# 72 of the 220 runs of edge rows are summed per tile inside the edge loop, the other 148 (listed as 150) in the summing pass behind it

## The reference, cut to what matters

```
h = concatenate([x[col], edge_attr], axis=1)      # col = dst, row = src
h = relu(h @ W1.T + b1)                           # 100,000 edges x 128
h = relu(h @ W2.T + b2)
summed = segment_sum(h, row, num_segments=n)      # per source node
cnt = segment_sum(ones, row, num_segments=n)
agg = summed / maximum(cnt, 1)
```

## Time and profile before

| | us |
|---|---|
| median of 3 runs | 3594.32 |
| the runs | 3587.15, 3594.32, 3613.79 |
| the profiled execution | 3586.66 |
| its span, first to last instruction | 3585.0 |
| mean granted clock of PE, share of full | 0.756 |

### The profile page before, as it was taken

One profiled execution on the slowest core, in us unless ns is written; L12 is line 12 of the kernel. 1 busy time (PEld: TensorE's weight loads), 2 busy tenths in 40 slices (PEclk: granted clock), 3 DMA queues, 4 the chain that ended last, 5 costly groups with the idle time before them and its releaser, 6 DMA issues. The chain is left out here.

```text
span 3585.0 us, 73734 instructions
## 1 busy us (share of the span) xinstructions
PE 2797.0 (78%) x15652; PEld 1906.7 (53%) x15653; DVE 2301.0 (64%) x7322; ACT 1370.4 (38%) x2945; POOL 1923.8 (54%) x1865
## 2 busy tenths in 40 slices
PE   7257777777777777545869988888898988885887
PEld 4146656665665666433333445555555555554875
DVE  7279999999999999657242235444444444443775
ACT  1045555555555555333000014444444444440001
POOL 0267777777777777530020006777777777773000
PEclk7556666656666656556879988888889788887998
DMA  4444444444444445881734322333333333334884
GB/s 138 86 122 120 136 125 115 126 127 116 120 137 113 120 119 102 70 121 52 217 104 129 109 63 69 84 82 80 82 82 81 80 82 80 82 79 132 253 256 121
DMA packets 584019, 404.72 MB, mean 113 GB/s; under 512 B 437776, under 2 KB 504643, under 8 KB 582916
## 3 DMA queue, kind: packets, MB, share of 16 engines
q1 hardware_dynamic: 449782, 133.68, 16.4%
q0 software_dynamic: 59344, 100.63, 13.9%
q10 hardware_dynamic: 74592, 167.22, 12.8%
HBM read 215.94 MB, written 210.09 MB: 119 GB/s over the span
## 5 line engine op out<-in xcount | busy, mean ns | idle before, releaser
L822 POOL DMA_INDIRECT at_hs<-table,at_rec_s x976 | 1050.3, 1076 | 409.0 <-issue 225.5
L2238 POOL DMA_INDIRECT edge_rows<-el_rows,el_idx x816 | 843.8, 1034 | 263.6 <-issue 232.0
L860 ACT CAST at_count_s<-near_ps 128x400 f16<-128x400 f32 x976 | 482.8, 495 | 754.8 <-PE near_ps L963 663.1
L963 PE MATMUL near_ps<-at_pair_hot,at_src_low_hot 128*128 128x425 f16 x976 | 477.7, 489 | 335.8 <-ACT at_count_s L860 274.7
L935 PEld LDWEIGHTS sums_ps<-at_hw,at_hit 128*128 128x128 f32 x1952 | 470.4, 332 | 34.0 <-issue 29.0
L935 PE MATMUL sums_ps<-at_hw,at_hit 128*128 128x66 f32 x1952 | 441.5, 408 | 8.4 <-DVE acc L1009 8.4
L963 PEld LDWEIGHTS near_ps<-at_pair_hot,at_src_low_hot 128*128 128x128 f16 x976 | 137.8, 141 | 444.5 <-ACT at_count_s L860 349.3
L1001 DVE TENSOR_SCALAR at_pair_hot<-iota_wide,at_rec_s 128x400 f16<-128x400 f16 x976 | 322.7, 333 | 0.1
L1009 DVE SCALAR_TENSOR_TENSOR acc<-acc,at_fade,sums_ps 128x66 f32 x976 | 266.5, 273 | 73.8 <-PE sums_ps L935 67.8
L2445 DVE TENSOR_TENSOR el_idx<-el_place,el_aside 128x8 uint32<-128x8 f32 x102 | 17.4, 171 | 454.0 <-DMA edge_rows<-el_rows,el_idx 453.7
L2522 PE MATMUL ts_sum_ps<-ts_rows,ts_hot 128*128 128x128 f32 x1760 | 221.9, 282 | 73.4 <-DVE ts_hot L2539 71.9
(11 more groups left out here) (404 smaller groups left out, 4599.9 us busy)
## 6 DMA issues: line engine op xcount, KB each, us to landing
slots<-at_count_s ACTq DMA_DIRECT2D x122, 850.0 KB
ts_rows<-edge_rows SPq DMA_DIRECT2D x110, 288.0 KB
ts_rows<-edge_rows ACTq DMA_DIRECT2D x110, 288.0 KB
el_rec<-attr SPq DMA_DIRECT2D x816, 32.0 KB
chunk<-slots SPq DMA_DIRECT2D x256, 100.0 KB
chunk<-slots ACTq DMA_DIRECT2D x208, 100.0 KB
attr<-in_edge_attr SPq DMA_DIRECT2D x16, 1248.0 KB
at_rec_s<-meta SPq DMA_DIRECT2D x976, 3.5 KB
```

The source lines that it names most:

```text
L822: pool.indirect_dma_start(hs[:, s, u, :], None, k.table, bass.IndirectOffsetOnAxis(rec[:, s, u, 0:1].bitcast(U32), 0)).then_inc(gathered[s ...
L860: a.copy(count[:, (n.o + d) % 2, i, 0:AW], near[:, (n.o + d) % 2, 0:AW]).then_inc(count_ready, 1)
L963: pe.matmul(near[:, s, 0:SW], low_hot[:, s, i, :], pair_hot[:, s, i, :], start=False, stop=True, skip_group_check=(i > 0)).then_inc(near_r ...
L2238: pool.indirect_dma_start(k.edge_rows, bass.IndirectOffsetOnAxis(idx[:, o % RECS, 4 * h + u:4 * h + u + 1], 0), rows[:, j, u, :], None).th ...
```

## The change

A unit that is full (all of its 512 rows are there) can be summed before the edge loop ends. The new code takes 72 full units (EARLY = (17 - 9 - 2) * 12) and sums them in the loop's last laps.

- After lap 8, DVE's `table()` works out from the running totals `run` how many full units each tile has, takes the first 72, and makes lists: rows of the 72 early units, and rows and tiles of the units that are left (up to 150, LATE). SP writes the six lists to DRAM and reads them back onto one partition (`quad_list`).
- In laps 10 to 15, ACT issues the loads of two early units at the end of each step (`load_quads`). One step later, DVE makes two `quad_hot` masks at its step's end (`quad_hots`); one after that PE makes the two sums, one in each half step between product1 and product2 (`sum_quads`); one after that DVE adds them to `k.sums` (`add_quads`, at its step's start, after two register reads). The pipeline drains in lap 16.
- To make room for two PSUM banks, `ea_ps` has one buffer instead of two, and PE waits for the previous half's copy before it transposes.
- `k.sums` is cleared by POOL before the edge loop's scatters instead of by DVE at the summing pass's start.
- The summing pass has 10 laps of 15 units with 6 row buffers. Since 15 is no multiple of 6 or 4, a unit's waits name the last user of its buffer in the lap before (`prior`).
- `finish_attention` no longer makes the unit lists (27 DVE steps and a memset fewer, 3 small steps more).
- The edge loop's code is written out in four laps and two hardware loops instead of two and one.

```diff
 RECS = 3
 EB = 6
-LAP = 20
-LOADS = 5
+TABLE_LAP = 9
+EARLY = (NB3 // EB - TABLE_LAP - 2) * 2 * EB
+LAP = 15
+LATE = -(-(Q2 - EARLY) // LAP) * LAP
+LOADS = 6
...
+            step(v.tensor_tensor_scan(unit_end[:], k.units[:], none[:], 0.0, ALU.add, ALU.add))
+            step(v.tensor_tensor(k.row_base[:], unit_end[:], k.units[:], ALU.subtract))
             step(v.tensor_scalar(k.row_base[:], k.row_base[:], float(UNIT), -1.0, ALU.mult, ALU.add))
             step(v.tensor_scalar(total[:], unit_end[:], -1.0, 0.0, ALU.add, ALU.max))
             step(v.tensor_scalar(total[:], total[:], float(UNIT), None, ALU.mult))
             step(v.tensor_copy(k.last_row[:], total[0:1, :]))
-            for t in range(NT):
-                step(v.scalar_tensor_tensor(tile_of[:], k.iota_wide[:, 0:Q2], unit_end[:, t:t + 1], tile_of[:], ALU.is_ge,
-                                            ALU.add))
-            step(v.tensor_copy(k.quad_tile[:], tile_of[0:1, :]))
-            step(v.tensor_scalar(tile_of[:], k.iota_wide[:, 0:Q2], float(UNIT), total[:, NT - 1:NT], ALU.mult, ALU.min))
-            step(v.tensor_copy(k.quad_row[:], tile_of[0:1, :]))
+            step(v.tensor_scalar(k.last_unit[:], unit_end[:, NT - 1:NT], -1.0, None, ALU.add))
+            for i in range(2):
+                step(v.tensor_scalar(k.iota_p2[:, i:i + 1], k.iota_p[:], float(P * i), None, ALU.add))
...
-        ea_ps = ps("ea_ps", [P, 2, CW])
+        ea_ps = ps("ea_ps", [P, CW])
...
+        quad_rows = sb("quad_rows", [P, LOADS, 4, HR])
+        quad_hot = sb("quad_hot", [P, 4, 4, P])
+        sum_ps = ps("sum_ps", [P, 2, CW])
...
+        def laps(eng, body, table=None):
+            body(0, True, False, None)
+            with eng.Fori(1, TABLE_LAP) as it:
+                body(it, False, False, None)
+            if table is not None:
+                table()
+            body(TABLE_LAP, False, False, None)
+            body(TABLE_LAP + 1, False, False, FIRST)
+            with eng.Fori(TABLE_LAP + 2, LAPS - 1) as it:
+                body(it, False, False, RUN)
+            body(LAPS - 1, False, True, DRAIN)
+
+        def slots(sums, o, lag):
+
+            if sums is None or (sums == FIRST and o < lag) or (sums == DRAIN and o >= lag):
+                return []
+            return [2 * (o - lag), 2 * (o - lag) + 1]
+
+        def nth(it, i):
+
+            return it * (2 * EB) + (i - 2 * EB * (TABLE_LAP + 1))
...
+                if not first and not last and sums is None and isinstance(it, int):
+                    sp.wait_ge(table_ready, 1)
+                    sp.dma_start(k.quad_dram.rearrange("i p -> p i"), found_i[:]).then_inc(table_written, 16)
+                    sp.wait_ge(table_written, 16)
+                    sp.dma_start(k.quad_list[:], k.quad_dram.rearrange("(a i) p -> a i p", a=1)).then_inc(list_loaded, 16)
...
+            nc.gpsimd.memset(k.sums[:], 0.0).then_inc(sums_clear, 1)
...
                 if not start:
-                    pe.wait_ge(ea_copied, q - 1)
+                    pe.wait_ge(ea_copied, q)
 
                 pe.sem_inc(passed, 1)
                 for u in range(4):
-                    t = pe.transpose(ea_ps[0:D, h, u * P:(u + 1) * P], rec[:, r, 4 * h + u, :], k.ident[:])
+                    t = pe.transpose(ea_ps[0:D, u * P:(u + 1) * P], rec[:, r, 4 * h + u, :], k.ident[:])
...
+            def sum_quads(it, some):
+
+                for i in some:
+                    pe.wait_ge(quad_hot_ready, nth(it, i + 1))
+                    if not (isinstance(it, int) and nth(it, i) < 2):
+                        pe.wait_ge(added, nth(it, i - 1))
+                    for r in range(4):
+                        m = pe.matmul(sum_ps[:, i % 2, 0:H], quad_hot[:, i % 4, r, :], quad_rows[:, i % LOADS, r, 0:H],
+                                      start=(r == 0), stop=(r == 3))
+                    m.then_inc(summed, 1)
...
                     product1(it, o, 1, now, False)
+                    due = slots(sums, o, 2)
+                    sum_quads(it, due[0:1])
                     product2(it, o, 0, start)
...
                         product1(it, o + 1, 0, now, False)
+                    sum_quads(it, due[1:2])
                     product2(it, o, 1, start)
...
+            def load_quads(it, some, at):
+
+                for i in some:
+                    if not (isinstance(it, int) and nth(it, i) < LOADS):
+                        act.wait_ge(summed, nth(it, i + 1 - LOADS))
+                        act.sem_inc(passed, 1)
+                    act.dma_start(quad_rows[:, i % LOADS].rearrange("p r f -> p (r f)"),
+                                  k.edge_rows[bass.ds(at[i], UNIT), :].rearrange("(p r) f -> p (r f)", p=P)
+                                  ).then_inc(quad_loaded[i % LOADS], 16)
+
+                if sums == FIRST:
+                    act.wait_ge(list_loaded, 16)
+                if sums in (FIRST, RUN):
+                    at = nc.values_load_multi_w_load_instructions(
+                        k.quad_list[0:1, 0, bass.ds(it * (2 * EB) - 2 * EB * (TABLE_LAP + 1), 2 * EB)],
+                        engines=[mybir.EngineType.Activation], min_val=0, max_val=JUNK - UNIT,
+                        skip_runtime_bounds_check_because="a row in front of the spare ones")[1]
...
+                    if sums in (FIRST, RUN):
+                        load_quads(it, slots(sums, o, 0), at)
...
+            def table():
+
+                step = Steps(dve, table_step)
+                step(v.memset(ones[:], 1.0))
+                step(v.memset(taken[:], 0.0))
+                step(v.tensor_tensor(count[:], run[:], k.row_base[:], ALU.subtract))
+                step(v.tensor_copy(full_i[:], count[:]))
+                step(v.tensor_single_scalar(full_i[:], full_i[:], 9, ALU.arith_shift_right))
+                step(v.tensor_copy(full[:], full_i[:]))
+                step(v.tensor_tensor_scan(ends_at[:, 0], ones[:], full[:], 0.0, ALU.mult, ALU.add))
+                step(v.tensor_tensor(count[:], ends_at[:, 0], full[:], ALU.subtract))
+                step(v.tensor_scalar(count[:], count[:], -1.0, float(EARLY), ALU.mult, ALU.add))
+                step(v.tensor_scalar(count[:], count[:], 0.0, None, ALU.max))
+                step(v.tensor_tensor(taken[:, 0:NT], count[:], full[:], ALU.min))
+                step(v.tensor_tensor(left[:], k.units[:], taken[:, 0:NT], ALU.subtract))
+                step(v.tensor_tensor_scan(ends_at[:, 0], ones[:], taken[:, 0:NT], 0.0, ALU.mult, ALU.add))
+                step(v.tensor_tensor_scan(ends_at[:, 1], ones[:], left[:], 0.0, ALU.mult, ALU.add))
+                for i, (w, c, more) in enumerate(((0, 0, left[:]), (1, 0, taken[:, 1:NT + 1]), (1, 1, taken[:, 1:NT + 1]))):
+                    at = k.iota_p2[:, c:c + 1]
+                    step(v.scalar_tensor_tensor(scrap[:], ends_at[:, w], at, ones[:], ALU.is_le, ALU.mult,
+                                                accum_out=found[:, i, 0:1]))
+                    step(v.scalar_tensor_tensor(scrap[:], ends_at[:, w], at, more, ALU.is_le, ALU.mult,
+                                                accum_out=found[:, i, 1:2]))
+                    step(v.tensor_tensor(found[:, i, 1:2], found[:, i, 1:2], at, ALU.add))
+                    if w:
+                        step(v.tensor_tensor(found[:, i, 1:2], found[:, i, 1:2], taken[:, 0:1], ALU.add))
+                step(v.tensor_tensor(found[:, :, 1], found[:, :, 1], k.last_unit[:].to_broadcast([P, 3]), ALU.min))
+                step(v.tensor_scalar(found[:, :, 1], found[:, :, 1], float(UNIT), None, ALU.mult))
+                step(v.tensor_copy(found_i[:, 0:3], found[:, :, 1]))
+                v.tensor_copy(found_i[:, 3:6], found[:, :, 0]).then_inc(table_ready, 1)
+            def quad_hots(it, some):
+                for i in some:
+                    dve.wait_ge(quad_loaded[i % LOADS], nth_load(it, i))
+                    if not (isinstance(it, int) and nth(it, i) < 4):
+                        dve.wait_ge(summed, nth(it, i - 3))
+                    v.tensor_tensor(quad_hot[:, i % 4], quad_rows[:, i % LOADS, :, H:H + 1].to_broadcast([P, 4, P]),
+                                    k.iota_row[:].unsqueeze(1).to_broadcast([P, 4, P]), ALU.is_equal).then_inc(quad_hot_ready, 1)
+            def nth_load(it, i):
+                per = 16 * (2 * EB // LOADS)
+                return it * per + (16 * (i // LOADS) + 16 - per * (TABLE_LAP + 1))
+            def add_quads(it, some, tiles):
+                for i, tile in zip(some, tiles):
+                    dve.wait_ge(summed, nth(it, i + 1))
+                    if not (isinstance(it, int) and nth(it, i) < 1):
+                        dve.wait_ge(added, nth(it, i))
+                    at = k.sums[:, bass.ds(tile, 1), :].rearrange("p t h -> p (t h)")
+                    v.tensor_tensor(at, at, sum_ps[:, i % 2, 0:H], ALU.add).then_inc(added, 1)
+            def body(it, first, last, sums):
+                if sums == FIRST:
```

(28 more changed lines are left out.)

83 lines of the change are left out of this document (50 added, 33 removed).

## The result

Measured side by side, the kernel before took 3587 to 3614 us in four executions and the changed one 3564.31 to 3576.86 us, median 3571.33 (five runs). A fifth execution of the kernel before took 3804 us, in a slower state that some executions show whatever the kernel, and is left out. The ratio is 0.9932, with a 95% interval of 0.991 to 0.9954: 0.7% faster, 24 us, where 1.7% and 60 us were forecast. The profiled execution after took 3576.86 us, with a span of 3575.2 and a mean granted clock of 0.752.

A forecast was written before the change was run, and what follows sets the result against it. POOL's scatters were taken to bound the edge loop, with the summing pass running alone after it. 3586.66 - 74 + 14 - 1 = 3526 us, and 7.7 more for the median, gave 3534 us, 1.7% faster, range 3505 to 3575.

The forecast's parts named there:

- What bounds the kernel: Edge loop: POOL's scatters bound it at 10.71 us a step; summing pass: runs alone, 257.9 us for 220 units.
- A lap is 9.7 + 8.9: Summing pass: a lap of 15 takes 18.6 us, stalled start plus nine sums; the pass 184 us, gain 74.
- 15 register reads (1.35 x 15 / 20 = 1.0): Summing pass, lap start: reading 15 tile numbers into registers costs 1.0 us plus gaps, scaled from 1.35 for 20.
- The clock: Summing pass: sums priced at PE's upper clock level, 0.99 us each, with nothing added for the lower level.
- The ring misfit: Summing pass: with 15 units and 6 buffers, loads 0 to 2 of a lap are ahead by three units, not five.
- Rival 5: Summing pass: lap starts cost the full 6.2 us, 216 us instead of 184, kernel 3566; chance 0.10.
- POOL, +14: Edge loop: early units' two masks a step delay POOL's scatters by 0.4 us in each of 36 steps, 14 us.
- rival 1: Edge loop: the masks cost POOL nothing, falling between scatters or not holding one; kernel 3520, chance 0.20.
- Hidden work: Edge loop: early units' work on PE (9.83 us a step against POOL's 11.1), DVE (2.3) and ACT costs no time.
- Rivals 2 to 4: Edge loop: PE becomes the bound, 3547 (0.12); PE's clock falls, 3662 (0.05); loads hold up scatters' landings, 3603 (0.08).
- POOL's clearing lies in its 15 us of waiting: Edge loop's start: POOL's clearing of `sums`, 2.9 us, falls in time POOL waits anyway and costs nothing.
- `finish_attention`, -1: In `finish_attention`: dropping the unit lists moves only the first addition, 1.0 us, out of the path; ends 0 and 2.5.

The follow-up runs named there:

- e5: Changed kernel with each lap's 15 list words starting 64 bytes apart, six row buffers and four masks kept; pass 219.6 us, ratio to the kernel before 0.9897.
- e6: Changed kernel with each lap's 15 list words starting 64 bytes apart, and five row buffers and five masks; pass 191.8 us, kernel 3524.43 us.
- e7: Kernel before with both unit lists stored one word (4 bytes) further on; pass 360.1 us, ratio to the kernel before 1.028.
- e2: Changed kernel, laps of 15 kept, with five row buffers and five masks so that both rings close; pass 218.2 us, kernel 3558.75 us.

## Why the prediction was wrong, point by point

**What bounds the kernel: right.** POOL bounds the edge loop before and after. In the pass the prediction looked for the cost at the lap starts, and it is there. Its nine units of each lap that "go at PE's pace" did so: 9.4 us where 8.9 was forecast.

**"A lap is 9.7 + 8.9": the step that failed is the 9.7,** the stretch from the end of unit 12's sum to the end of the next lap's unit 3. It took 14.0 us. In the prediction's own terms, as means over the nine lap starts, in us from the end of unit 12's sum:

| | forecast | after | e5, reads aligned |
|---|---|---|---|
| mask of unit 2 ends | 6.6 | 8.1 | 8.4 |
| from there to the end of unit 3's mask (VectorE's read) | 2.1 | 3.9 | 2.5 |
| from there to the end of unit 3's sum | 1.0 | 2.0 | 2.0 |
| the other nine sums | 8.9 | 9.4 | 9.1 |
| lap | 18.6 | 23.4 | 22.0 |

Three terms were too small. "15 register reads (1.35 x 15 / 20 = 1.0)" made the cost proportional to the words; it was 1.55 us in three laps and 3.39 in seven, and the queues' reads (3.08 and 3.23) were not in the sum at all. The third load and its mask came 1.5 us later than "near 5.9" and 6.6. And the sums were all priced at TensorE's upper clock level, 0.99 us, while unit 3's ran at the lower one in seven of the nine laps. The lap came to 23.2 us (231.7 / 10), and the gain to 29.6 instead of 74. Of the missing 44, e5 gives back 12.1. So the slow reads are the surprise, but not the larger part: with every read aligned and the ring as the prediction had it, the pass is still 219.6 us, where 184 and the 3.4 from the first load's issue to the first mask make 187.

**The clock: a term put at nothing.** The mean granted clock over the pass was 0.98 before and 0.82 after; with levels of 1 and 0.5 that is 36% of 231.7 us at the lower one. The trace has 268 of the 1,200 matmul records in it. Eight of them take 1.87 us there and 0.99 at the upper level, so the clock cost at most 268 / 8 x 0.88 = 29 us, if every one of them was waited for. How much it was is open. It is hardly a cause of its own, for each of the nine lap starts, where TensorE had stood, has a fall of the clock in it, but it makes each stall dearer, and differences between the runs above have it in them: the mean was 0.85 in e5, 0.95 in e6 and 0.79 in e7.

**The ring misfit: the mechanism right, its size not settled.** DVE does wait for loads 0 to 2, and PE stands 2.12, 0.63 and 2.37 us there. Closing the row buffers' ring gives 13.5 us with slow reads and 27.8 without; the model's stall was (18.6 - 15 x 0.99 - 1.0) x 9 = 25. Rival 5, "the lap starts cost the full 6.2 us", had laps of 22.3 and a time of 3566, and so came nearest to the 23.2 and 3571; but that is luck, for it had the whole of it in the ring, where e2 shows that closing the ring is worth 1.35 a lap as long as the reads are slow.

**POOL, +14: too much.** It was 2 to 3.4 us. The scatters that began under a mask ended 0.84 or 0.85 us after it, as forecast, but a hold came to 6.6 / 36 = 0.18 us and not 0.4, and the sum took each as added, where the time under `miss` fell by 5.8. The scatter's mean is 298.51 / 286 = 1.044 in the laps with masks, where 1.09 was forecast and 1.035 stood before. By its price for the masks rival 1 was near, by its reason (the masks fall between scatters, or do not hold one) not.

**Hidden work: right.** PE, 2 sums a step: busy 0.95 of the time at a clock of 0.96; the steps stayed at 385.5 / 286 x 8 = 10.78 us. DVE's standing before `idx` fell from 170.6 to 84.8 us in the 380 us from 2838 on, 2.4 us a step where 2.3 was forecast, and was not used up. Rivals 2 to 4 did not come: the clock rose, as argued, and the loads held up no landing that anyone waited for. One price in it was wrong without harm: the two-word reads take 0.53 us a step and not 0.14.

**"POOL's clearing lies in its 15 us of waiting": wrong by 1.2 to 4.6 us.** POOL had the time, but DVE and, through the first `miss`, PE did not.

**`finish_attention`, -1: it was 0.** The removed 12 us lay beside transfers; DVE now stands for them.

```profile
1692.20 1.02 DVE L1188 TENSOR_TENSOR pre<-pre,att_summed 128x832 f32<-128x832 f32 x1 [4.33 <-DMA att_summed<-by_group]
...
1701.57 0.96 DVE L1188 TENSOR_TENSOR pre<-pre,att_summed 128x768 f32<-128x768 f32 x1 [8.35 <-DMA att_summed<-by_group]
```

In the earlier trace rows the two additions followed each other directly. From the chain's first step that both kernels have (`src_total`) to the end of the second addition it is 17.2 us in both traces of the kernel before, 17.4 here, and 16.8 to 18.2, mean 17.3, over the twelve changed kernels. In the changed kernels the second addition waits for its transfers; before, the chain happened to end just as they had landed. The first addition moved forward without moving the end.

**The sum with measured terms:** 3585.0 - 29.6 + 3.0 + 3.4 + 0.7 + 1.4 = 3563.9 of span, 0.6% under before, without the 11.3 us that vary from run to run.

## What to carry to other kernels

When a lap's length changes, recount what is paid once a lap on every queue, and look at the start address and the length of each list that registers are read from: with 60 bytes a lap seven of ten lists begin off a multiple of 16, and that cost 12 to 26 us of the 74 that the pass was to gain. Before crediting units with being "already loaded", divide the buffers' round trip by their number: here 1.17, 1.09 and 0.90 us a unit for 5, 6 and 12 buffers. Price sums behind a stall at the lower clock level too. And two stalls at one place must be taken away together, and not only one by one, before either is judged.
